# Gated unit of a feed-forward layer: two of the three passes after the matmuls move from GpSimd to VectorE, and ScalarE's copy of the gate goes

## The reference, cut to what matters

```python
gate = _matmul_lora(x, gate_w, gate_a, gate_b)
up = _matmul_lora(x, up_w, up_a, up_b)
hidden = jax.nn.silu(gate) * up
out = _matmul_lora(hidden, down_w, down_a, down_b)
```

## Time and profile before

| what | value |
|---|---|
| median of 3 runs | 928.84 us |
| lowest to highest | 928.5 to 931.58 us |
| the profiled execution's own time | 929.51 us |
| its span, from first to last instruction | 927.8 us |
| TensorE (PE) matmul busy | 882.7 us, 95% |
| VectorE (DVE) busy | 574.6 us, 62% |
| ScalarE (ACT) busy | 488.4 us, 53% |
| GpSimd (POOL) busy | 345.2 us, 37% |
| mean granted TensorE clock | 0.988 of full |

### The profile page before, as it was taken

The page is one execution under the profiler, slowest core; times in us unless marked ns, Lnnn a source line. Parts: engine busy times, 40 slices in busy tenths (PEclk is TensorE's granted clock), DMA queues, the critical chain, the costliest instruction groups (busy, mean ns, idle before and its releaser), DMA issues.

```text
span 927.8 us, 21796 instructions
## 1 busy us (share of the span) xinstructions
PE 882.7 (95%) x8415; PEld 643.3 (69%) x8415; DVE 574.6 (62%) x1674; ACT 488.4 (53%) x1002; POOL 345.2 (37%) x340
## 2 busy tenths in 40 slices
PE   3988699999999999999999999999999999999997
PEld 3764477676767777776767777665677777787885
DVE  6666375766665757565666666677766667651136
ACT  3432365656565656565666565656645454545211
POOL 4152236363635354544445454432121313130133
PEclk9999799999999999999999999998999999999999
DMA  8465525343434343434343535356565546434664
GB/s 279 156 198 167 146 66 145 80 143 82 139 90 133 96 134 97 131 94 128 88 133 78 143 84 146 84 145 184 191 219 158 167 133 194 155 99 137 213 206 136
DMA packets 143094, 129.80 MB, mean 140 GB/s; under 512 B 37360, under 2 KB 115920, under 8 KB 140816
## 3 DMA queue, kind: packets, MB, share of 16 engines
q1 hardware_dynamic: 142992, 128.41, 47.6%
HBM read 74.09 MB, written 53.74 MB: 138 GB/s over the span
## 4 chain that ended last, share of the span: by engine, by line
PE 87%; DVE 4%; DMA 3%; ACT 2%; SPq 2%; issue 2%; DVEq 0%; ACTq 0%
PE bank L1096 27%; PE bank L1140 15%; PE o L1278 14%; PE s L1242 9%; PE st L1261 8%; PE bank L304 3%; PE bank L305 2%; PE bank L306 2%; PE bank L1059 1%; PE bank L1105 1%; DMA scratch_k<-proj_hi 1%; DMA sums<-scratch_o 1%; PE bank L1074 1%; SPq L966 1%; PE s L1249 1%
## 5 line engine op out<-in xcount | busy, mean ns | idle before, releaser
L1543 ACT ACTIVATE prob<-st 128x512 f32<-128x512 f32 (+1 forms) x640 | 323.5, 554 | 260.9 <-PE st L1261 259.5
L1808 DVE CUSTOM_DVE_ANT_0 junk<-s,mask 128x128 bf16<-128x128 f32 (+3 forms) x512 | 229.1, 486 | 80.0 <-PE s L1242 79.4
L1811 DVE TENSOR_REDUCE part_max<-s 128x1 f32<-128x512 f32 x256 | 164.0, 682 | 126.7 <-PE s L1242 126.3
L1242 PE MATMUL s<-k,q 64*128 64x512 f32 (+3 forms) x768 | 157.9, 375 | 15.1 <-DMA q<-scratch_q 7.0
L1096 PE MATMUL bank<-x_hi,w_hi 64*128 64x512 f32 (+1 forms) x704 | 151.7, 414 | 1.3 <-DVE proj_lo L1629 0.8
L602 POOL TENSOR_SCALAR_AFFINE_SELECT prob<-prob 128x512 f32<-128x512 f32 x128 | 80.8, 643 | 181.0 <-ACT prob L1543 180.7
L1278 PE MATMUL o<-prob,v 128*32 128x512 f32 (+3 forms) x1536 | 145.4, 497 | 0.0
L1096 PE MATMUL bank<-x_lo,w_hi 64*128 64x512 f32 (+1 forms) x704 | 144.2, 393 | 0.0
L1096 PE MATMUL bank<-x_hi,w_lo 64*128 64x512 f32 (+1 forms) x704 | 143.6, 391 | 0.0
L1261 PE MATMUL st<-q,k 64*128 64x512 f32 (+3 forms) x768 | 141.9, 345 | 0.2 <-DMA q<-neg_rows 0.2
L1242 PEld LDWEIGHTS s<-k,q 64*128 64x128 f32 x768 | 80.8, 186 | 52.0 <-DVE part_max L1808 22.2
(11 more groups left out here) (156 smaller groups left out, 1175.3 us busy)
## 6 DMA issues: line engine op xcount, KB each, us to landing
late_context_hid_in<-scratch_hid SPq DMA_DIRECT2D x16, 1408.0 KB, 6.9
q<-scratch_q SPq DMA_DIRECT2D x60, 200.0 KB
scratch_hid<-tanh_hid_hi SPq DMA_DIRECT2D x40, 256.0 KB, 2.4
scratch_hid<-hid_lo SPq DMA_DIRECT2D x40, 256.0 KB, 3.0
scratch_o<-o_sb SPq DMA_DIRECT2D x32, 256.0 KB
scratch_q<-proj_hi SPq DMA_DIRECT2D x30, 256.0 KB
k<-scratch_k SPq DMA_DIRECT2D x30, 192.0 KB
x_again<-in_L_attn_x SPq DMA_DIRECT2D x16, 256.0 KB, 5.0
```

Source lines behind the costliest of these rows:

```text
L1242: pe.matmul(sb_[(p + odd) % S_BANKS][:, 0:wd], q[half, g % 2, h // 2, qt * P:(qt + 1) * P], k[half, g % 2, k0:k0 + wd], start=True, stop=T ...
L1543: nc.scalar.activation(prob[:, job % 3, h, 0:JOB_COLS[j]], st[at % ST_BANKS][:, 0:JOB_COLS[j]], ACT.Exp, scale=float(HD) ** -0.5).then_inc ...
L1808: ins = dve.tensor_tensor_reduce(junk[:, n % S_BANKS, 0:wd], bank_[:, 0:wd], mask[:, C - wd:C], 1.0, LOWEST, ALU.add, ALU.max, part[:, h, ...
L1811: ins = dve.tensor_reduce(part[:, h, qt, dst:dst + 1], bank_[:, 0:wd], AX.X, ALU.max)
```

## The change

ScalarE no longer copies the gate; it takes the tanh alone, out of `bank[0]`. VectorE waits for the tanh, then writes (tanh + 1) * gate out of `bank[0]`, waits for its own result, and multiplies it by 0.5 and by up out of `bank[1]`. GpSimd's `finish` is gone. `hid_done` is replaced by `up_read`, which now comes with the finished tile, and TensorE waits for `up_read` alone. The tile `gs` goes. The GpSimd program keeps its count of steps, so all that remains stands where it stood.

```diff
-                gs = sbuf(own, "gate", [P, C])
...
             if kind == "hidden":
-                return (gate_read, NCH * a + b + 1), (up_read, NCH * a + b + 1)
+                return (up_read, NCH * a + b + 1),
...
-            def finish(h, c):
-                hp, n = rows[h], NCH * h + c
-                pool.wait_ge(gate_read, n + 1)
-                pool.wait_ge(up_read, n + 1)
-                pool.tensor_tensor(th[0:hp, n % 2], th[0:hp, n % 2], hid[0:hp, n % 2], ALU.mult).then_inc(tanh_used, 1)
-                pool.wait_ge(tanh_used, n + 1)
-                pool.tensor_tensor(hid[0:hp, n % 2], th[0:hp, n % 2], hid[0:hp, n % 2], ALU.add).then_inc(hid_done, 1)
-
             def low_hidden(h, c):
                 hp, n = rows[h], NCH * h + c
                 pool.wait_ge(hid_hi, n + 1)
-                pool.wait_ge(hid_done, n + 1)
...
                         if c >= 2 and h + 1 < NH:
                             low_weight(h + 1, c - 2)
-                        yield STEPS["hidden"] - KT
-                        done += STEPS["hidden"] - KT
-                        finish(h, c)
-                yield sum(FOLD_STEPS[:2])
+                yield STEPS["hidden"] - KT + sum(FOLD_STEPS[:2])
...
                 wait_filled(act, key)
-                if n:
-                    act.wait_ge(up_read, n)
-                nc.scalar.activation(gs[0:hp], bank[0][0:hp, :], ACT.Copy, scale=0.5).then_inc(gate_copied, 1)
                 if n >= 2:
                     act.wait_ge(hid_stored[n % 2], 2 * DMA * (n // 2))
                 nc.scalar.activation(th[0:hp, n % 2], bank[0][0:hp, :], ACT.Tanh, scale=0.5).then_inc(gate_read, 1)
...
             def split_hidden(n):
                 hp = rows[n // NCH]
-                act.wait_ge(hid_done, n + 1)
+                act.wait_ge(up_read, n + 1)
...
-                dve.wait_ge(gate_copied, n + 1)
-                dve.tensor_tensor(hid[0:hp, n % 2], bank[1][0:hp, :], gs[0:hp], ALU.mult).then_inc(up_read, 1)
+                dve.wait_ge(gate_read, n + 1)
+                dve.scalar_tensor_tensor(out=hid[0:hp, n % 2], in0=th[0:hp, n % 2], scalar=1.0, in1=bank[0][0:hp, :],
+                                         op0=ALU.add, op1=ALU.mult).then_inc(gated, 1)
+                dve.wait_ge(gated, n + 1)
+                dve.scalar_tensor_tensor(out=hid[0:hp, n % 2], in0=hid[0:hp, n % 2], scalar=0.5, in1=bank[1][0:hp, :],
+                                         op0=ALU.mult, op1=ALU.mult).then_inc(up_read, 1)
```

More of the change, by code:

```diff
@@ L459, in layer @@
         up_read = sem("up_read")
-        tanh_used = sem("tanh_used")
-        gate_copied = sem("gate_copied")
-        hid_done = sem("hid_done")
+        gated = sem("gated")
         hid_hi = sem("hid_hi_done")
```

## The result

The changed kernel took 940.59 us in the median (938.12 to 941.8, four runs), the kernel before 928.67 us beside it; the ratio is 1.0131, with a 95% interval of 1.0096 to 1.0166. The forecast was 941.5 us. The span of the profiled execution grew from 927.8 to 940.1 us. One execution in experiment 3 and one in experiment 5 took 4603.82 and 2068.02 us; the medians count them, the ratios and their intervals don't.

The account below looks back on a forecast made before the run. TensorE, 87% of the chain, was taken as the bound, with its waits at bank hand-overs deciding. Per block 0.725 and 0.425 make 1.15 us, over 11 blocks 12.65; span 927.8 becomes 940.45, median 941.5 us, range 934 to 950.

Parts of the forecast that it names:

- VectorE starts when it did: At each hand-over of the two banks: VectorE's first operation still starts 0.73 us after ScalarE's start; cost nothing.
- The hold grows by 0.725 us: At each hand-over: VectorE's second operation waits for its first, so both banks come free 0.725 us later.
- c = 3 pays 0.725 us: One of a block's four hand-overs: TensorE already waits for VectorE there, so it pays the whole 0.725 us.
- c = 0 pays 0.425 us: One of a block's four hand-overs: 0.30 us of the longer hold is covered, so TensorE pays 0.425 us.
- c = 1 and c = 2 pay nothing: A block's other two hand-overs: slack of 0.77 and 0.80 us covers the delay, by 0.04 and 0.08 us.
- rival 2: At the hand-overs: the hold is longer than the rows say and all four pay; 949.0 us, chance 0.13.
- The maxima behind `hid` cost nothing: VectorE's queue behind each hand-over: maxima come 0.725 us later without delaying TensorE, 0.18 us to spare at the tightest.
- ScalarE's relief is worth nothing: ScalarE loses 44 copies of 0.60 us: no gain taken, up to 5.7 us kept as a bound.
- GpSimd's relief is worth nothing: GpSimd loses 88 operations of 1.29 us; VectorE gets back 0.98 us once a block, worth nothing to TensorE.
- Rival 3: In the hidden-unit stage: TensorE really waits for VectorE, held by GpSimd; 10.8 us come back, 918.0 us, chance 0.04.
- Rivals 1 and 4: Hand-overs: first, only c = 3 pays, 936.8 us, chance 0.09; fourth, later release costs little, 929 us, chance 0.03.
- DMA waits of `proj_lo`: VectorE's wait for sums delays `proj_lo`, costing TensorE 4.2 us in four places; may vanish or double, so range only.

Follow-up runs that it names:

- experiment 3: Against the kernel before: VectorE copies up times 0.5 during the tanh, then does (tanh + 1) * gate; ScalarE's copy gone, GpSimd keeps one product; 926.3 us, ratio 0.9989.
- experiment 5: Kernel before plus one VectorE operation of only 128 columns, out of the up bank behind the product; 931.08 us, ratio 1.0026; run again for its timeline, 929.77 us.
- experiment 6: Against the kernel before: VectorE only copies up, without waiting for ScalarE, and GpSimd does the three remaining passes; 926.61 us, ratio 0.9977.
- Experiment 7: The changed kernel with TensorE again waiting for two semaphores, gate_read and up_read, instead of one; 940.39 us, ratio 1.0115.
- Experiment 4: The changed kernel with VectorE's first operation done twice, each waiting for the one before; 966.37 us, ratio 1.0418.
- experiment 2: The changed kernel with VectorE's pair cut to one operation, (tanh + 1) * up, leaving out gate and 0.5; 926.25 us, ratio 0.9987.
- experiments 1: The kernel before plus a second full-size VectorE operation out of the up bank, waiting for the product and signalling in its place; 941.41 us, ratio 1.0149.

## Why the prediction was right, point by point

- **VectorE starts when it did**: 0.73 us behind ScalarE in both kernels, but for one hand-over of the changed kernel, with 1.09. Right in the main.
- **The hold grows by 0.725 us**: 0.72 us from start to start, both operations 0.69. Right, at the rows' price. The estimate of 65 ns more for a PSUM source that follows from the Trainium skill (VectorE: DVE Perf Modes, "The TRN2 errata") is not seen in this trace: 689 ns with a PSUM operand, 688 without.
- **c = 3 pays 0.725 us**: 0.71. Right, and experiment 6 shows why there was nothing to cover it: TensorE arrives at 1.45 us and was let in at 1.54. (The second place that was read, lies six blocks later, not seven.)
- **c = 0 pays 0.425 us**: 0.35. This term was mis-sized. The forecast took 0.12 us from VectorE's end to the load, as at c = 3; it was 0.05, because the change also takes one of TensorE's two waits away, which the section on the change names and the prediction put at nothing without a reason. Experiment 7 gives most of it back. Eleven times 0.07 us is 0.8 of the forecast's 12.65.
- **c = 1 and c = 2 pay nothing**: right in 21 of 22 cases, with margins that were as thin as written. The late VectorE at c = 1 of the third block cost 0.3 us, which is rival 2's mechanism in one place; the prediction had named such growth as a sign of being wrong. Experiment 4 shows both paying as soon as the hold goes past the slack.
- **The maxima behind `hid` cost nothing**: right, 13.4 against 13.7 us.
- **ScalarE's relief is worth nothing**: right; the waits for `prob` are 5.7 us in both.
- **GpSimd's relief is worth nothing**: right for TensorE. VectorE did get its 0.98 us back behind c = 0, from 1.16 to 0.18, and experiment 2 shows that it changes no time. Rival 3 fell by this.
- **Rivals 1 and 4**: both fell at the hand-overs, as c = 0 paid 0.35 us and c = 3 paid 0.71.
- **DMA waits of `proj_lo`**: 4.2 us at the weight loads before, 2.7 in the changed kernel, 6.9 in experiment 5, none in experiments 2 and 3. What makes them come and go was not tried. The prediction read the 4.2 us as TensorE's loss, and that was too much: PE itself waited 0.8 us for `proj_lo` before and 0.9 in the changed kernel. The term was not in the sum; it widened the range at the low end.
- **The sum**: 11 x (0.71 + 0.35) = 11.7 us, against 12.65 forecast; the span grew by 12.3. The mechanism was right. That the total came out nearer to the forecast than the hand-overs alone is chance in part: the late c = 1 gave 0.3 us and the stretches outside the stage 0.4.

## What to carry to other kernels

Where a pair of banks is handed between engines without a second pair, look at each hand-over's own slack: the distance from the last reader's end to the consumer's next load, less the shortest such distance in the trace. (That shortest distance differed by 0.07 us here with the number of waits.) In this kernel a longer hold cost what exceeded that slack, hand-over by hand-over, whatever the busy shares were; moving 112 us of work off GpSimd, for which TensorE did not wait, bought nothing. If a pass must be added, put a part that needs no other engine's result first, beside the work that is waited for anyway.

## What the runs showed of the hardware that was not expected

- The way from VectorE's last operation to TensorE's next weight load has two lengths here. It is 0.05 us where one wait stands before the load (c = 0 in the changed kernel, c = 2 in experiment 4) and 0.11 to 0.12 us where two stand there (c = 0 in experiments 1 and 7). At c = 3, and at c = 1 in experiment 4, it is 0.11 to 0.12 us although only one wait is for the banks; waits for weights stand before those loads as well, which fits, but they were not removed by themselves. The kernel before has both lengths elsewhere: where score loads, with two waits, are held, they start 0.12 us behind the end of VectorE's maximum, and loads for transposed scores, with one, 0.05 us behind ScalarE's exponential (medians).
- VectorE's operations on 128 x 512 float32 out of PSUM took 0.68 to 0.69 us whether copy, scale, product or scalar_tensor_tensor. What differs is the distance to the next: 0.72 us where it waits for the first one's result, and 0.60 us where its wait is over by then (c = 0 of experiment 3, starts at 305.46 and 306.06 us). The 0.63 us at c = 3 of experiment 3 is set by the tanh, which ends 0.03 us before the second operation starts.
